# Four chained attention blocks on one core: all four engine orders replaced, output added in memory order, output stored in halves

## The reference, cut to what matters

```python
# L0
mm1 = softmax(einsum('bci,bcj->bij', xr, xr)); mm2 = einsum('boi,bij->boj', w_conv @ xr, mm1)
x = einsum('bcs,bsj->bcj', relu(w_gap @ mean_pool(x)), mm2) + x
# L1: q, k, v are 1x1 convolutions with batch norm (16, 16 and 128 channels)
attn = softmax(einsum('bci,bcj->bij', q, k)); x = gamma * einsum('bcj,bij->bci', v, attn) + x
# L2: neighbours in space (3x3 without the middle) and in channels
h_s = softmax(where(adj, alpha.T @ sigma, NEG)) applied to x; h_p = softmax(where(cadj, x @ x.T, NEG)) @ x
x = (1 - gama) * x + gama * elu(h_s + h_p)
# L3: 16 projected channels, 2-D FFT, energy by angle in 90 bins, two peaks, gain per frequency, inverse FFT
fs = fft2(w_in @ x); energy = segment_sum(mean(|fs|) * high_mask, bin_idx); peaks = top_k(energy, 2)
x = x + w_out @ real(ifft2(fs * gain(peaks)))
```

## Time and profile before

| | us |
|---|---|
| three timed runs | 338.33, 340.81, 340.81 (median 340.81) |
| the profiled execution | 339.55 |
| its span, first to last instruction | 337.8 |
| mean granted clock of PE | 0.937 of full |
| busy: PE, PEld, DVE, ACT, POOL | 305.0, 214.1, 243.1, 196.3, 60.3 |
| HBM read, written | 5.83 MB, 2.10 MB |

### The profile page before, as it was taken

One profiled execution on the slowest core, in us unless ns is written; L12 is line 12 of the kernel. 1 busy time (PEld: TensorE's weight loads), 2 busy tenths in 40 slices (PEclk: granted clock), 3 DMA queues, 4 the chain that ended last, 5 costly groups with the idle time before them and its releaser, 6 DMA issues.

```text
span 337.8 us, 4453 instructions
## 1 busy us (share of the span) xinstructions
PE 305.0 (90%) x1545; PEld 214.1 (63%) x1545; DVE 243.1 (72%) x369; ACT 196.3 (58%) x365; POOL 60.3 (18%) x51
## 2 busy tenths in 40 slices
PE   2999997999879899999999999989989998976794
PEld 2767543857657677685666484656957577854473
DVE  3796579678898779838799845888675876053784
ACT  3355679468489476854685746759764494052120
POOL 1123000234412441002000002441028500000000
PEclk9999998599979999999999989999799999587599
DMA  7930000000000000000000000000000000000014
GB/s 213 390 87 2 1 1 2 0 0 0 2 0 0 0 3 0 2 1 2 0 0 2 1 0 0 2 1 0 3 0 0 0 3 2 0 0 0 2 65 186
DMA packets 3544, 8.22 MB, mean 24 GB/s; under 512 B 910, under 2 KB 1550, under 8 KB 3522
## 3 DMA queue, kind: packets, MB, share of 16 engines
q1 hardware_dynamic: 3522, 7.93, 6.7%
HBM read 5.83 MB, written 2.10 MB: 23 GB/s over the span
## 4 chain that ended last, share of the span: by engine, by line
PE 33%; issue 32%; DVE 17%; ACT 8%; POOL 7%; DMA 1%; DVEq 0%; ACTq 0%; POOLq 0%
PE psum L331 32%; DVE e1l L866 6%; POOL e1h L977 6%; ACT psum L629 3%; ACT e L638 2%; DVE nmax L846 1%; DVE nmax L801 1%; PE psum L416 1%; DMA xin<-in_x 1%; DVE qs L836 1%; DVE ks L834 1%; POOL xin L980 1%; DVE qs L863 1%; POOL xl L971 1%; ACT ks L612 1%
## 5 line engine op out<-in xcount | busy, mean ns | idle before, releaser
L977 POOL CAST e1h<-e 128x1024 fp32r<-128x1024 f32 x32 | 43.2, 1360 | 107.4 <-ACT e L638 102.6
L866 DVE TENSOR_TENSOR e1l<-e,e1h 128x1024 fp32r<-128x1024 f32 x32 | 41.8, 1321 | 15.2 <-POOL e1h L977 15.0
L801 DVE TENSOR_REDUCE nmax<-psum 128x1 f32<-128x1024 f32 x32 | 38.8, 1223 | 13.0 <-PE psum L331 12.1
L599 ACT ACTIVATE e<-psum,nmax 128x1024 f32<-128x1024 f32 x32 | 35.6, 1114 | 21.2 <-PE psum L331 8.6
L629 ACT ACTIVATE psum<-psum,nmax 128x1024 f32<-128x1024 f32 x32 | 34.8, 1088 | 14.9 <-DVE nmax L846 14.7
L638 ACT ACTIVATE e<-psum 128x1024 f32<-128x1024 f32 x32 | 32.1, 1023 | 17.8 <-DVE e1l L866 15.4
L846 DVE TENSOR_REDUCE nmax<-psum 128x1 f32<-128x1024 f32 x32 | 37.8, 1219 | 3.7 <-PE psum L331 3.5
L331 PE MATMUL psum<-ks,qs 96*128 96x512 f32 (+2 forms) x96 | 30.0, 407 | 6.2 <-ACT psum L629 5.2
L331 PE MATMUL psum<-xh 128*128 128x512 f32 x64 | 28.8, 450 | 6.4 <-DVE xl L792 6.0
L331 PE MATMUL psum<-e,v0n 128*64 128x512 f32 x128 | 30.6, 610 | 0.0
L331 PE MATMUL psum<-qs,ks 96*128 96x512 f32 (+2 forms) x96 | 27.8, 394 | 1.3 <-ACT e L638 0.6
(11 more groups left out here) (165 smaller groups left out, 562.3 us busy)
## 6 DMA issues: line engine op xcount, KB each, us to landing
xin<-in_x SPq DMA_DIRECT2D x4, 512.0 KB, 5.8
out<-xin SPq DMA_DIRECT2D x4, 512.0 KB, 2.7
twist<-in_twist_in SPq DMA_DIRECT2D x1, 768.0 KB, 7.4
zz<-in_region_in SPq DMA_DIRECT2D x2, 360.0 KB, 5.8
untwist<-in_untwist_in SPq DMA_DIRECT2D x1, 512.0 KB, 7.4
bins<-in_bins_in SPq DMA_DIRECT2D x1, 372.0 KB, 7.3
zz<-in_near_in SPq DMA_DIRECT2D x1, 288.0 KB, 4.4
rw<-in_rows_w SPq DMA_DIRECT2D x1, 256.0 KB, 3.0
```

The costliest lines, as they stand in the source:

```text
L599: inc(go(e0[:, E0_AT[b, i], :], t[:, :], ACT.Exp, bias=nmax0[z][:, i:i + 1], accum_out=sum0[z][:, i:i + 1]), "e0_ready", b)
L801: inc(vec.tensor_reduce(nmax0[z][:, i:i + 1], t[:, :], AX.X, ALU.max, negate=True), "nmax0_ready", b)
L866: inc(vec.tensor_tensor(e1l[:, EH_AT[b, i], :], e1[:, E1_AT[b, i], :], e1h[:, EH_AT[b, i], :].bitcast(F32), ALU.subtract), "e1l_ready", b)
L977: inc(gp.tensor_copy(e1h[:, EH_AT[b, i], :], e1[:, E1_AT[b, i], :]), "e1h_ready", b)
```

## The change

Three things. All four lists, and the banks in `PE_TEXT`, are other permutations of the same steps. `y.b.i` now covers half of the image's pixels in memory order: `xin` is read and written in order and PSUM at a distance of 128 values, and both `y` of an image wait for both `wout`. SP stores each half as soon as its `y` is done, 256 KB at a time. Two more lines in the file shift the line numbers behind it by 2, those of `y` by 3 (L946 is L949).

```diff
 PE_TEXT = (
-    "gram.0.0@0 gram.0.1@2 gap.0.0@4 xconv.0.0@5 gram.0.2@6 gram.0.3@0 gram.0.4@2 gram.0.5@4 gram.0.6@6 "
+    "gap.0.0@0 xconv.0.0@1 gram.0.0@2 gram.0.1@4 gram.0.2@6 gram.0.3@0 gram.0.4@2 gram.0.5@4 gram.0.6@6 mix.0.0@0 "
...
 DVE_STEPS = steps(
-    "split.0.0 split2.0.0 bn1.0.0 pool.0.0 gram.0.0 gram.0.1 bn2.0.0 gram.0.2 gram.0.3 gram.0.4 norm0.0.0 "
+    "split.0.0 pool.0.0 split2.0.0 bn1.0.0 pool.1.0 gram.0.0 gram.0.1 gram.0.2 gram.0.3 norm0.0.0 gram.0.4 "
...
             for b in range(B):
-                wait(sp, "y_ready", b, 1)
-                sp.dma_start(out[b], xin[:, b, :]).then_inc(out_written, 16)
-            sp.wait_ge(out_written, 16 * B)
+                for h in range(2):
+                    hc = slice(h * HALF, (h + 1) * HALF)
+                    wait(sp, "y_ready", b, h)
+                    sp.dma_start(out[b][:, hc], xin[:, b, hc]).then_inc(out_written, 16)
+            sp.wait_ge(out_written, 16 * 2 * B)
...
                 elif name == "y":
-                    wait(dve, "y_full", b, i)
+                    wait(dve, "y_full", b, 1)
                     wait(dve, "x3_ready", b, 1)
-                    tv = tile(("wout", b, 0))[:, hc].rearrange("p (j r) -> p j r", r=P)
-                    xv = xin[:, b, :].rearrange("p (r j) -> p j r", j=CH)[:, 4 * i:4 * i + 4, :]
+                    rows = slice(i * P // 2, (i + 1) * P // 2)
+                    tv = tile(("wout", b, 0)).rearrange("p (j r) -> p r j", r=P)[:, rows]
+                    xv = xin[:, b, hc].rearrange("p (r j) -> p r j", j=CH)
                     inc(vec.tensor_tensor(xv, tv, xv, ALU.add), "y_ready", b)
```

## The result

The changed kernel took **325.22 us** (median of 4 runs, 323.29 to 326.84); the kernel before, in the same session, 339.57 (337.17 to 340.81). The ratio is 0.9583, 95% interval [0.9499, 0.9667]. The profiled execution took 323.29 us with a span of 321.5, against 339.55 and 337.8. The forecast was 326.0.

A forecast was written before the change was run, and what follows sets the result against it. TensorE was taken as the engine to look at, losing time to waits and reduced clock. From the profiled 339.55 us, -9.5 for the body and -4.0 for the end game gave 326.0 us, range 318 to 332 (chance 0.58).

The forecast's parts named there:

- the body: Everything up to the last shift transposes at 282.0 us: reordered steps save 13.5 us, hand-overs cost 4.0, net -9.5.
- the end game: Everything behind the last shift transposes: +0.6 ahead of xproj.3, -4.1 behind it, -0.5 from half stores, together -4.0 us.
- The pieces: Eight stretches cut where PE runs the shift transposes, each priced by work and time on the chip; sum -13.5 us.
- the marks that the forecast listed as a sign: Times of the eight shift transposes if right: about 64, 99, 126, 157, 193, 224, 252 and 268 us.
- the +4.0 for hand-overs: Score and scoreT tiles alternating: 0.25 us for each of 16 tiles of images 0 and 2, range 0 to 10.4.
- e1l: DVE's subtraction for each scoreT tile, 1.32 us behind 1.36 of GpSimd; leading PE's waits would show the forecast wrong.
- The first piece: Start to first shift transposes: +1.5 late gram, -6 fewer score waits and half clock, +3.1 PE work; net -1.0 us.
- The sixth and seventh pieces: Stretches before the sixth and seventh shift transposes: -12.3 and +4.6 us, together -7.7, where the prediction is most exposed.
- A: Rival: each alternating tile pays the full 0.65 us hand-over and eats the body's gain; 332 to 336 us, chance 0.15.
- B: Rival: balanced pieces two to four, six and seven run at the worst factor, 1.25; 343.5 us, slower, chance 0.10.
- C: Rival: PE's clock stays up once the gaps go, giving another 10 us; 316 us, chance 0.08.
- D: Rival: the order does nothing, only y and half stores count, 2 us; 337.5 us, chance 0.09.

The follow-up runs named there:

- e2_order_only: The changed kernel's four orders with the y additions and whole-image stores of the kernel before: 326.12 us, ratio 0.9625 to the kernel before.
- e3_new_end: The kernel before with only its end-game steps in the changed order, y and stores as before: 341.57 us, ratio 1.0094.
- e5_fill_end: The changed kernel plus 32 products that nobody reads in TensorE's end-game waits: 324.66 us, ratio 0.9609 to the kernel before.

## Why the prediction was right

**The sum.** 326.0 forecast and 325.22 measured, but its two parts missed in opposite directions: in the profile the body gave -14.5 instead of -9.5, the end game -1.8 instead of -4.0. The sum started from the profiled 339.55 us, and the profiled execution of the changed kernel took 323.29, 2.7 less than forecast. That the median lies 0.8 us off is in part luck: errors of 5.0 and 2.2 us against each other, and a profile faster than the median.

**The body, piece by piece.** The pieces were forecast at 35, 27.5, 31, 36, 31, 28 and 16 us behind the first and came out at 35.7, 26.1, 29.8, 32.8, 30.5, 29.7 and 15.6. In sum that is 200.2 us for 204.5 forecast, with misses of up to 3.2 us in single pieces. The method, PE's or DVE's work of the piece, whichever is heavier, times a factor, held in that sense. Not all factors were today's: 1.10 and 1.17 were chosen where the second and sixth pieces show 1.18 and 1.25 (37.6 / 32.0, 43.3 / 34.6); 1.13 and 1.15 came. Before hand-overs the sum was -13.5, nearly the answer, and the marks that the forecast listed as a sign, up to 268, are of that sum; with its own +4.0 the eighth would stand at 272.5. It came at 267.5. **The step that failed is the +4.0 for hand-overs**: with the alternation DVE's wait before `e1l` fell from 15.0 to 3.5 us, ScalarE's wait for `e1l` from 15.4 to 7.2, and PE's from 1.5 to 1.2.

The first piece was the other miss: counted from 6 us as in the forecast, its mark came after 61.3 us instead of 58.0. The head had been priced at +1.5; the run with the old head puts it at 2.0 us. With that and the 3.1 us more of PE work the scores among mixes gave about 2.8 us (an estimate, 59.0 + 2.0 + 3.1 - 61.3) and not 6, as much as the pair of moves in the kernel before gave at its first mark.

Two sums of the forecast don't come out of its own figures, without an effect on the total beyond 0.4 us: the heavier engines of the pieces add up to 241.5 and 232.3 us, not to 262 and 235, and the first piece to 57.6, not to 58.0.

**Why the body gains** is shown only in part. Where it gains can be read: up to the eighth mark PE is busy 254.1 us instead of 263.0 and idle 6.1 instead of 13.0 (summed over the stretches), and it starts 1.3 us later: -8.9 - 6.9 + 1.3 = -14.5. Of the 8.9, 6.6 are clock (lengths times what is missing to 1.00: 10.2 us before, 3.6 now). Of the 6.9, 5.7 stood ahead of the score products, 6.2 us before and 0.5 now. That is what the forecast had named as the loss, and the fall of the clock near 56 us is gone as it expected. But that the waits bring the clock down isn't shown by it, and the single pair of moves in the kernel before gave 2.8 us at the first mark, 2.1 at the end of its profile, and nothing that can be told in the median. The sixth and seventh pieces together went from 66.7 to 60.2 us, -6.5 against the -7.7 on which the forecast was said to rest. No run splits the body further than that; which of its moves carry the rest stays open.

**The end game.** The pick under `xproj.3` came as said: the second pick starts 13.4 us behind the start of that step, against about 13 forecast. The part ahead of `xproj.3` had been taken at +0.6, the price of `pick.0.0` ahead of x3 less the shorter waits, and came out at +0.5 (19.47 us for 18.93). **What was over-priced is the part behind it**, -4.1 with y and -0.5 for the store, against -2.3 measured (34.5 us for 36.9). Still, the pick ahead of x3 buys nothing: the run with it moved back starts `xproj.3` 1.3 us earlier. The two runs with the new order but the old y and stores (e2_order_only and e3_new_end) both take 35.4 us behind `xproj.3`: the order gave 1.5 us there instead of 2.5, y and halves 0.9 instead of 2.1. y had been taken at 0.70 and is 0.686, so it isn't its length. What may cost is that each y now waits for both `wout` halves, which the forecast called felt by `y.0.0` alone; no run tries that by itself. From the start of `wout.3.0` to the end the new y and halves take 7.0 us (321.5 - 314.5) and the old ones 7.3 (338.3 - 331.0, in the run with the new end alone), the shorter landing included: the span ends 2.6 us behind the last y. The clock goes the same way: half from 310.4 us on, where the kernel before had its full rate from 319.3 to 336.3. With the waits filled (e5_fill_end) the part behind `xproj.3` takes 33.5 us, so the clock is about 1.1 of the 2.3 us that were missing; the rest no run splits.

**The rivals.** A fell with the hand-overs. B needed a factor of 1.22 in pieces two to four, six and seven; they took 151.8 us for 135.7 of PE's work, 1.12. C took the clock as rising: the mean went only from 0.937 to 0.946, since it rose in the first two pieces but fell in the end game, from 0.80 (282.0 to 337.8 us) to 0.74. D fell too, but its 2 us for y and halves without the order needs a y at another place: put in as it is, it makes the kernel of before 2.3% slower. The forecast had the wait of `y.0.0` for `wout.0.1` and put it at 0.8 us; what it did not see is that the copy of `selT.1` stands behind it in the order of before, with the clock at stake.

## What to carry to other kernels

Price each stretch by the heavier of its engines times a factor that the same kernel shows. Before adding a price for a hand-over, look whether the engine that gets more to do stands idle there today: DVE had 15.0 us of waits in which the score's reduction could stand. Before putting a wait for a whole tile where one for half a tile stood, look at what is queued behind it: moving one word here was worth 2.9% of the kernel's time. And ask of each stretch whether TensorE's work or a chain of small steps sets it: filling the waits to keep the clock up gave 4.7 us in the end game where the work was packed at the end, and 1.1 us where the chain led.

## What the hardware showed that I had not expected

- VectorE reads float32 from PSUM 512 bytes apart as fast as in order, 686 against 683 ns for 512 columns; the same distance put on the SBUF side, read and written 32 bytes apart, costs 1088. The Trainium skill (Advanced Engine Details and Errata, Memory Cachelines) has a pattern in PSUM that isn't contiguous slow down matmuls; this access is VectorE's, and there the measurement shows no cost.
- TensorE's granted clock fell right behind or during the `xproj` steps of images 0, 1 and 2 in the changed kernel (at 197.7, 221.6 and 272.8 us), sixteen matmuls of 16 columns in which PE is marked busy (3.75 us at 193.52, 3.88 us at 268.34), and for image 3 already in the wait ahead of it. So the clock fell here while or right after the profile marked PE busy.
- At half clock, 14.09 us of PE work in 18.2 us did not bring the clock back; in the kernel before 12.90 us in 17.0 (319.3 to 336.3) ran at full clock all through, and of its 127 matmuls the last 73 are the same as there.
- The run-to-run spread of the kernel before (336.59 to 342.5 us over 16 runs) goes with its mean clock, 0.947 down to 0.928.
